# Hybrid SSD, attention and selective-scan block on one core: one feature copy handed to VectorE, the gelu turn of the layers reordered, and the first steps of the next pair formed ahead in the scan

## The reference, cut to what matters

```python
x = x + attn_a(layernorm(x))   # SSD: projection, short convolution, chunked state space, gate
x = x + ffn(layernorm(x))      # two layers of local attention and a gated feed forward
x = x + attn_b(layernorm(x))   # selective scan: 256 channels x 16 states, step by step over the tokens
x = x + ffn(layernorm(x))      # the same two layers again, same weights

# one layer of ffn
h = shift_token(x); q, k, v = split(h @ wqkv)               # 8 heads of 64
q = l2norm(q) * qs; k = l2norm(k) * ks; q, k = rotary_xpos(q, k)
x = x + local_attention(q, k, v) @ wo                       # window 64
h = layernorm(shift_token(x)) * lg + lb
a, g = split(h @ w1 + b1)                                   # 341 + 341 hidden
x = x + (a * gelu(g)) @ w2 + b2

# attn_b, per channel and state
state = A_bar * state + B_bar * B * x;  out = sum_over_states(state * C)
y = layernorm(out * silu(z)) @ Wout
```

## Time and profile before

| | us |
| --- | --- |
| three executions | 2657.2, 2639.4, 2646.31 |
| their median | 2646.31 |
| the profiled execution, its own time | 2651.16 |
| its span, first to last instruction | 2649.4 |
| TensorE busy | 2192.8 (83%) |
| VectorE busy | 1996.1 (75%) |
| ScalarE busy | 1856.4 (70%) |
| GpSimd busy | 1543.0 (58%) |
| mean granted TensorE clock | 0.928 |

### The profile page before, as it was taken

The page is one execution under the profiler, slowest core; times in us unless marked ns, Lnnn a source line. Parts: engine busy times, 40 slices in busy tenths (PEclk is TensorE's granted clock), DMA queues, the critical chain, the costliest instruction groups (busy, mean ns, idle before and its releaser), DMA issues. The chain is left out here.

```text
span 2649.4 us, 46209 instructions
## 1 busy us (share of the span) xinstructions
PE 2192.8 (83%) x13308; PEld 1124.7 (42%) x13308; DVE 1996.1 (75%) x5421; ACT 1856.4 (70%) x4745; POOL 1543.0 (58%) x1364
## 2 busy tenths in 40 slices
PE   5888789999999999667777767776799899999997
PEld 2555445455555555222222222222355455555553
DVE  4666477777777776388998989898677777787774
ACT  3555277778777777488687777776677777777774
POOL 1233276556665665177787677676565556665652
PEclk8999799999999999788888888889999999999999
DMA  3000000000000000000000000000000000000000
GB/s 129 1 0 1 4 13 13 10 14 12 13 13 14 12 9 14 0 0 1 1 1 1 0 1 0 0 1 0 13 13 13 9 14 12 13 17 17 21 13 17
DMA packets 12209, 30.04 MB, mean 11 GB/s; under 512 B 2240, under 2 KB 2240, under 8 KB 11584
## 3 DMA queue, kind: packets, MB, share of 16 engines
q1 hardware_dynamic: 11968, 27.41, 3.8%
HBM read 8.52 MB, written 2.10 MB: 4 GB/s over the span
## 5 line engine op out<-in xcount | busy, mean ns | idle before, releaser
L517 POOL TENSOR_TENSOR arena<-arena 128x512 f32<-128x512 f32 x256 | 325.0, 1270 | 444.8 <-DVE arena L1530 444.8
L575 POOL TENSOR_TENSOR arena<-arena 128x512 f32<-128x512 f32 x256 | 327.7, 1295 | 127.2 <-ACT arena L1257 118.5
L523 POOL TENSOR_TENSOR arena<-arena,SR 128x512 f32<-128x512 f32 x256 | 285.3, 1114 | 109.5 <-ACT SR L1139 108.6
L1610 DVE TENSOR_TENSOR_SCAN arena<-arena,psum 128x512 f32<-128x512 f32 x256 | 311.0, 1215 | 3.2
L929 PE MATMUL psum<-BS,tabs 96*128 96x512 bf16 x384 | 146.1, 442 | 197.1 <-DVE arena L1610 195.3
L997 PE MATMUL psum<-arena,first 128*128 128x512 f32 x512 | 288.8, 653 | 10.9 <-POOL arena L566 10.6
L1536 DVE TENSOR_REDUCE SM<-arena 128x8 f32<-128x512 f32 x256 | 175.6, 686 | 155.9 <-ACT arena L1129 145.5
L530 POOL TENSOR_TENSOR P<-P,RS 128x512 f32<-128x512 f32 x256 | 270.3, 1056 | 35.5 <-DVE RS L1457 35.1
L1129 ACT ACTIVATE arena<-psum 128x512 f32<-128x512 f32 x256 | 151.4, 591 | 186.6 <-PE psum L853 186.5
L853 PE MATMUL psum<-rest,HA 128*128 128x512 f32 x512 | 267.3, 604 | 0.4 <-DVE HA L1445 0.4
L807 PE MATMUL psum<-HN,rest 128*128 128x512 f32 (+1 forms) x384 | 197.0, 640 | 56.0 <-ACT arena L1122 51.0
(11 more groups left out here) (223 smaller groups left out, 5290.8 us busy)
## 6 DMA issues: line engine op xcount, KB each, us to landing
arena<-arena SPq DMA_DIRECT2D x128, 128.0 KB, 2.3
rest<-in_rest SPq DMA_DIRECT2D x1, 4183.0 KB, 20.9
X<-in_x SPq DMA_DIRECT2D x1, 2048.0 KB, 9.0
out<-X SPq DMA_DIRECT2D x8, 256.0 KB, 2.3
tabs<-in_tabs SPq DMA_DIRECT2D x1, 1216.0 KB, 11.5
first<-in_first SPq DMA_DIRECT2D x1, 875.5 KB, 4.5
```

The lines of the kernel that those rows point to most:

```text
L517: nc.gpsimd.tensor_tensor(CQ[:, n % 2, :], CQ[:, n % 2, :], SQN[:, n % 2, :], ALU.add).then_inc(f_rope, 1)
L523: nc.gpsimd.tensor_tensor(heads, heads, SR[:, n % 2, :].unsqueeze(2).to_broadcast([128, HEADS, DH]), ALU.mult).then_inc(f_qk, 1)
L575: nc.gpsimd.tensor_tensor(WU[:, k % DEEP, :], RG[:, k % DEEP, :], U[t.j % 2][:, k % 2, :], ALU.mult).then_inc(m_wu, 1)
L1610: v.tensor_tensor_scan(HS[:, k % DEEP, :], AB[:, k % DEEP, :], B_BANK[k % 2], 0.0, ALU.mult, ALU.add).then_inc(m_hs, 1)
```

## The change

Five edits. In the layers: (1) the feature copy of the fourth item (h = 21) is made by VectorE in turn 5, behind its `flipped` copy, instead of by ScalarE behind the gelus; (2) TensorE's gate half 2 and other half 0 move from h = 21 to h = 23, behind `project` of item 5 (h = 22), and VectorE's `gated(0)` moves from h = 22 to h = 25; (3) in every turn ScalarE issues `norms` ahead of `features`. In the scan: (4) the first two `WU` of the next pair, its first two `spread_b` and first `spread_c` are issued in the turn of the pair before, ahead of the last `odd_times_c` and the last three `accumulate`; (5) VectorE's centring, normalised input and `WV`/`PV` of the next pair go one step later (k = 2, 8, 11 become 3, 9, 12).

```diff
@@ GpSimd, scan
+            def weighted_input(t, k, pair=0):
+                t.wait_ge(m_rg, STEPS, k + 1, pair=pair)
+                t.wait_ge(m_vb, STEPS, k + 1 - DEEP, pair=pair)
+                if k == 0:
+                    t.wait_ge(m_u, 1, 1, pair=pair)
+                nc.gpsimd.tensor_tensor(WU[:, k % DEEP, :], RG[:, k % DEEP, :], U[(t.j + pair) % 2][:, k % 2, :],
+                                        ALU.mult).then_inc(m_wu, 1)
...
-                        t.wait_ge(m_rg, STEPS, k + 1)
-                        t.wait_ge(m_vb, STEPS, k + 1 - DEEP)
-                        if k == 0:
-                            t.wait_ge(m_u, 1, 1)
-                        nc.gpsimd.tensor_tensor(WU[:, k % DEEP, :], RG[:, k % DEEP, :], U[t.j % 2][:, k % 2, :],
-                                                ALU.mult).then_inc(m_wu, 1)
+                        if k >= 2:
+                            weighted_input(t, k)
...
-                if t.states:
-                    odd_times_c(t, NS - 2)
-                    odd_times_c(t, NS - 1)
+                for late in range(2):
+                    if t.after:
+                        weighted_input(t, late, pair=1)
+                    if t.states:
+                        odd_times_c(t, NS - 2 + late)
@@ TensorE, layers
-                    elif h == 21:
+                    elif h == 23:
                         gate_half(k, 2)
                         other_half(k, 0)
@@ TensorE, scan
                 if t.states:
-                    spread_b(t, 0)
-                    spread_c(t, 0)
-                    spread_b(t, 1)
                     spread_c(t, 1)
...
-                    if t.states and k >= 2:
+                    if t.states and 2 <= k < STEPS - 1:
                         accumulate(t, k - 2)
+                if t.after:
+                    spread_b(t, 0, pair=1)
+                    spread_c(t, 0, pair=1)
+                    spread_b(t, 1, pair=1)
                 if t.states:
-                    accumulate(t, STEPS - 2)
-                    accumulate(t, STEPS - 1)
+                    for k in range(STEPS - 3, STEPS):
+                        accumulate(t, k)
@@ ScalarE, layers
-                if item(k, h, 7):
-                    features(k, *item(k, h, 7))
                 if item(k, h, 3):
                     norms(k, *item(k, h, 3))
+                if item(k, h, 7) and h // 4 != 5:
+                    features(k, *item(k, h, 7))
@@ VectorE, layers
+            def features(k, m, n):
+                tt, part = divmod(n, 2)
+                k.wait_ge(f_xp, 8, n + 1, slot=m)
+                v.tensor_copy(QKT[k.side(m)][:, 4 * part:4 * part + 4, 128 * tt:128 * tt + 128],
+                              T_BANK.rearrange("p (c t) -> p c t", t=128)).then_inc(f_qkt, 1)
...
-                    elif h == 22:
+                    elif h == 25:
                         gated(k, 0)
...
+                    if g == 5 and item(k, 21, 7):
+                        features(k, *item(k, 21, 7))
@@ VectorE, scan (dve_beginning)
-                if k == 2:
+                if k == 3:
                     t.wait_ge(ln_mean, 1, LN_M + 1, pair=1)
...
-                elif k == 8:
+                elif k == 9:
                     t.wait_ge(ln_rs, 1, LN_M + 1, pair=1)
...
-                elif k == 11:
+                elif k == 12:
                     t.wait_ge(m_exp, 1, 1, pair=1)
```

More of the change, by code:

```diff
@@ L926, in _, with spread, spread_b, spread_c @@
             pe.wait_ge(f_x, PAIRS)
-            def spread(t, s, column, dst, done):
-                mm(dst, T16("sel", 128 * column, 128 * column + 128, p=96), BS[t.j % 2][:, :],
+            def spread(t, column, dst, done, pair):
+                mm(dst, T16("sel", 128 * column, 128 * column + 128, p=96), BS[(t.j + pair) % 2][:, :],
                    start=True, stop=True).then_inc(done, 1)
-            def spread_b(t, k):
-                t.wait_ge(m_hs, STEPS, k - 1)
+            def spread_b(t, k, pair=0):
+                t.wait_ge(m_hs, STEPS, k - 1, pair=pair)
                 if k == 0:
[L935 to L940, removed]
+                    t.wait_ge(m_bs, 3, 3, pair=pair)
+                spread(t, k // 2, B_BANK[k % 2], m_bb, pair)
+            def spread_c(t, s, pair=0):
+                t.wait_ge(m_pce, NS, s - 1, pair=pair)
+                spread(t, NS + s, C_BANK[s % 2], m_bc, pair)
             def half_sum(k, weight, source, done):
```

## The result

The changed kernel takes 2662.4 us (median of 15 runs, 2654.3 to 2666.7), the kernel before 2651.7 us in the same rounds (15 runs, 2639.4 to 2661.0). The ratio is 1.0035 with an interval of 1.0019 to 1.0051: slower by 9 us, inside the 1% that counted as no change. The forecast was 2663 us. The agreement is better than the working: the forecast was +17 us on a median of 2646.3 us in three runs, which in fifteen is 2651.7, and the measured difference is +9 (5 to 14). So it has to be looked at term by term.

What follows compares the result with a forecast made beforehand. TensorE bounds the layers, VectorE the scan. Layers +29 us and scan -12 (19.3 gained, 7 lost) give +17: 2663 us against the median 2646.3; own bounds 2637 to 2684, with B and part of A 2625 to 2695.

Steps and rivals of the forecast that it cites:

- Edit 1: Layers, gelu turn: the copy takes 0.66 us in VectorE's idle time; norms, squares and sums come 0.50 us earlier.
- Edit 2: Layers, gelu turn: other half 2 waits for gated(0), next project 1.0 us later; 28 slots, 28 us longer.
- The sum of the layers: Both layer phases together: 29 us longer, 28 slots at 1.0 us plus 1 us for the other turns.
- Edit 3: Layers, turns other than the gelu turn: zero, with bounds of -3 to +3 us over both phases.
- Edit 4: Scan, ends of pairs: VectorE's idle time between pairs mostly goes, 19.3 us gained, bounds 14 to 23.
- The 2 us left at the loop's return: Scan: at each of two loop returns 2 us of waiting were left standing, bounds 0 and 4.6 us.
- Edit 5: Scan: centring about 1.5 us later, 7 us lost; L1651's 17.9 us of waiting turns into waits for GpSimd.
- The clip: Scan, VectorE's L1669: counted as unchanged; it took 0.745 us once and 5.26 in the median of eight.
- A: Layers: the hold by gated(0) doesn't decide, 0.9 us a slot gained, 25 us; 2609 us in all; chance 0.17.
- B: Layers: TensorE's clock falls in more slots, from 20 slots on at 1.5 us: +30, 2693 us; chance 0.14.
- C: Scan: shifted waits make the five long clips short, 18 us, 2645 us, or the short ones long, +7; chance 0.11.
- D: Scan: edit 4 is ineffective, accumulates hold VectorE's L1622 instead, so 19.3 us stay: 2682 us; chance 0.08.

Runs made afterwards that it cites:

- copy_only: Kernel before with only edit 1 (fourth item's feature copy on VectorE): 2633.4 us, ratio to before 0.9956.
- gated_23: The changed kernel with VectorE's gated(0) at h = 23 instead of h = 25: 2615.1 us, ratio to before 0.9873.
- layers_only: Kernel before with only edits 1 to 3, scan as it was: 2663.4 us, ratio to before 1.0072.
- copy_norms: Kernel before with only edits 1 and 3: 2641.3 us, ratio to before 0.9954.
- norms_only: Kernel before with only edit 3 (norms ahead of features on ScalarE): 2652.5 us, ratio to before 1.0023.
- ahead_only: Kernel before with only edit 4 (first steps of the next pair ahead): 2629.0 us, ratio to before 0.9918.
- g23_ahead: The changed kernel with gated(0) at h = 23 instead of 25 and edit 5 undone: 2606.1 us, ratio to before 0.9829.
- scan_only: Kernel before with only edits 4 and 5, layers as before: 2637.9 us, ratio to before 0.9957.
- late_only: Kernel before with only edit 5 (next pair's preparation one step later): 2660.3 us, ratio to before 1.0040.
- edit2_only: Kernel before with only edit 2 (gate half 2 and other half 0 at h = 23, gated(0) at h = 25): 2682.4 us, ratio 1.0152.
- best_no5: g23_ahead with the clip L1669 written as a scalar_tensor_tensor, same result: 2610.8 us, ratio to before 0.9853.
- clip_24: g23_ahead with VectorE's clip at k = 24 instead of 20 and ScalarE's Ln at k = 27 instead of 24: 2614.9 us, ratio 0.9890.

## Why the prediction was right, and where it wasn't

**Edit 1** held: copy 0.68 us for 0.66, hidden in VectorE's idle time, squares and sums earlier by 0.48 us for 0.50. copy_only shows that this is all that edit 1 gives, 0.5 us a slot. (The prediction speaks of "the SBUF-only clip of edit 5"; the clip is L1669, which edit 5 leaves in its place.)

**Edit 2** held in every event of the table above to 0.04 us. The 1.0 us a slot is the 0.98 between the two periods, made of 1.47 for the hold less 0.5 for edit 1. What decided the sign was that `gated(0)` would stand behind sums, products, `output` and the first `maxima`, and that nothing later absorbs it; gated_23 shows it.

**The sum of the layers failed in size.** The forecast was +29; the profile has +23 (the fourteen slots of either phase, from the first load, +11.0 and +12.0), the timed layers_only +19 (12 to 26). The failed step is that 28 slots at 1.0 us were summed with the clock left as it was. In before, seven slots had a fall, a usual slot then lasting 46.16 us and not 45.48; in after none had. These seven grew by 0.07 to 0.32 us instead of 0.99, 5.3 us less together, and 27.7 - 5.3 = 22.4. The other 21 grew by 0.9 to 1.2 us but for two, by +2.8 (a fall of after, 28 us behind the load) and -0.3 (one of before, 25 us behind it), which leaves the 23.0 of the profile.

**Edit 3** was put at zero with bounds of 3. Beside edit 1 that is right within what can be told (copy_norms 0.9954, copy_only 0.9956). Alone it costs 6 us (1 to 11), 0.17 us a slot; 28 such are 4.8. The cost alone lies around the gelu turn: TensorE's attention behind it waits 0.9 us for the copy instead of 0.5 (norms_only), and in the change ScalarE has no copy left there.

**Edit 4** held: 19.3 us forecast, 22 (14 to 29) by ahead_only, 20.8 by the gaps between pairs in after (28.7 less 7.9), and 23.3 by the scans of before and g23_ahead (706.6, 683.3), which have two short clips each (see below). What the scan gains beyond the gaps I didn't follow. The 2 us left at the loop's return came out as 1.6 to 1.9.

**Edit 5** was put at 7 us. The profiles of scan_only and ahead_only, both with seven long clips, differ by 7.4 us in the scan (696.6, 689.2); the gates come 0.3 to 1.5 us later in the eight pairs, 6.8 us together. The claim that L1651's 17.9 us would turn into waits for GpSimd is what the runs show: in after 14.6 us fewer at its successor (17.9 to 3.3), and L1619's wait for GpSimd rose from 14.6 - 9.2 = 5.4 to 20.7, by 15.3. "The centring comes about 1.5 us later" is what before and after show, 9.83 us behind the pair's first recurrence for 8.36 in the usual pair, and late_only too. Beside edit 4 it is 2.3 (7.53 in ahead_only), since there the 0.75 us of waiting are gone already. By the timed runs edit 5 seems to cost more than 7: 11 us (7 to 15) in late_only, 10 between ahead_only and scan_only, 12 between g23_ahead and gated_23. But in the first and the last pair of kernels part of it is the clip: late_only's scan is 11.4 us longer than before's (718.0, 706.6) and gated_23's 13.5 longer than g23_ahead's (696.8, 683.3), and in both cases the longer one has no short clip and the other has two. At 3.3 to 4.6 us each (below) that leaves 2 to 5 and 4 to 7 us for edit 5.

**The clip** was put at no change, and that is the step that failed in the scan. Durations of the seven clips inside the scan, one profiled execution of each kernel:

| scan | kernels | short (1.6 us) |
|---|---|---|
| as before | before 2, copy_only 2, copy_norms 3, edit2_only 3, norms_only 4, layers_only 5 | 19 of 42 |
| edit 4, 5 or both | after 2, g23_ahead 2, scan_only 0, ahead_only 0, late_only 0, gated_23 0 | 4 of 42 |

A pair with a short clip is 3.3 us shorter (85.7 and 89.0 us in after). Over the whole scan it is up to 4.6: scan_only and gated_23, with the scan of after and no short clip, have 696.6 and 696.8 us, after with two 687.6. Before and after happen to have two short clips each in their profiled executions, so these two compare like with like: the scan is 19.0 us shorter, against 12 forecast. But an average execution of the old scan has 3.2 short clips by this table and one of the new 0.7: 2.5 times 3.3 to 4.6 is 8 to 12 us given back, which leaves 7 to 11 of the 19; scan_only's timed runs give 11 (7 to 16). So the forecast of -12 was met in part by luck, by an edit 4 a little better than forecast and by short clips that became long. With one execution a kernel the counts are small: they run from 2 to 5 in the old kind of scan and from 0 to 2 in the new, and the 8 to 12 us are an estimate.

**The rivals.** A (the hold doesn't decide, 2609 us) is excluded for after. Without the hold gated_23 comes near its time, 2615, but by 0.5 us a slot and fewer falls and not by A's 0.9. B (the clock falls more) had its sign wrong: 7 slots became none. C (the clip) was thought of in the wrong direction, 18 us gained against 7 lost; the lost side is what happened. (Its 3.7 us a clip are 5.26 less the 1.6 us of the short clips in the scan, which the earlier trace rows doesn't show; the 0.745 there is the clip ahead of the scan.) D (edit 4 ineffective) is excluded by the gaps.

On B, the counts go with edit 2: the six other kernels with `project` ahead of the gate halves (layers_only, edit2_only, gated_23, g23_ahead, best_no5, clip_24) have no fall behind the gelus, like after; the six without it besides before (copy_only, copy_norms, norms_only, scan_only, ahead_only, late_only) have 7 to 9. That is the good side of edit 2: beside edit 1 a usual slot with a fall lasts 46.16 us and not 45.00, and copy_norms has nine, about 10 us. gated_23 is 21 us below copy_norms by the ratios, of which 11 are the scan's. In the first kind TensorE's longest wait in the turn is 1.2 or 1.3 us, in the second it is the 1.7 to 2.0 us at the gelus. That the length of that single wait matters, and not their sum (0.83 + 1.17 + 1.24 = 3.2 us in after), is what these counts suggest; that it is the cause was not tried by itself. The Trainium skill's page "TensorE: Matmul & The Clock Gate", section "A second HAM failure mode: psum-queue depth-cycling", has frequent short idle times as what makes the clock swing. In these runs more and shorter idle times gave fewer falls.

## What to carry to other kernels

When an operation is moved later in a hand-written order, follow the operations that it now stands behind to the one that was waiting on data: `gated(0)`, 0.75 us long, moved three half turns, stood behind sums that ScalarE could not give earlier, and cost 1.47 us in each of 28 turns, while the good half of the change was worth 0.5. Two edits that come in one change are to be priced apart, since a version with the one slot put back was faster than either kernel (2606 us with edit 5 out as well). And a stall that sits in one instruction may belong to the place and not to it: see where it goes when the instruction is moved before its time is counted as a gain; clip_24 gained nothing by making every clip short, because a subtraction of 0.68 us took the stall over.

## What the runs showed of the hardware

- A VectorE instruction of 0.69 us (the 128x1024 clip, one input, SBUF to SBUF) lasted 5.26 us in most pairs, one of 1.27 us (the same with two inputs) 5.8 in three of seven, and one of 0.68 us (32x512, two inputs in SBUF) 5.83 in five of seven in clip_24 and 1.14 or 1.32 in the scans of the other kernels. The first and the third end 0.55 us after GpSimd's row of instructions without a gap, the second 1.08 us after it. The Trainium skill, page "Advanced Engine Details and Errata", section "VectorE Performance Modes", has GpSimd and two-port VectorE instructions block each other; the clip agrees. By that section alone I had not expected the subtraction to wait: ahead of the scan it takes 0.68 us with both inputs in SBUF, and with one in PSUM 0.68 everywhere, so it is no faster for having both there. Its PSUM form, the recurrences (1.21 to 1.22 us in after) and the products with B (0.67 to 0.70), which all have an operand in PSUM, never lasted longer, though 197 of the 256 recurrences of after began while GpSimd was at work.
- Sometimes the same clip gets in between two GpSimd instructions: at 1292.10 in after it took 1.59 us, and GpSimd's next instruction took 1.74 us instead of 1.25. What decides between 1.6 and 5.3 us is open. Kernels with the same scan differ in how often each comes (after 2 short of 7, gated_23 and scan_only none), and one clip is 3.3 us of its pair.
- The usual slots of the second layer have the same length to 0.03 us in different kernels wherever the clock doesn't fall (46.46 to 46.48 in after and layers_only, 44.98 to 45.01 in gated_23, copy_only and clip_24). The 0.17 us a slot of edit 3 were plain there, where the time of the whole kernel only just told them (1.0005 to 1.0041).
